# Half of the head sums moved to TensorE in a fused attention and mixture-of-experts block

## The reference

```python
scores = einsum('bhqd,bhkd->bhqk', q, k) / sqrt(DK)
attn = softmax(scores, axis=1)             # axis 1 is the HEAD axis
x = einsum('bhqk,bhkd->bhqd', attn, v)     # then times Wo
# the block: x = x + attention(layernorm(x), ctx)
#            x = x + ffn(layernorm(x))
raw = einsum('bsd,ed->bse', x, centroids)  # routing scores, top 2 of 8, softmax of the two
h_sh = gelu(x @ Wfc_sh);  shared_out = h_sh @ Wproj_sh
h_r = gelu(x @ Wfc_r);    expert_out = h_r @ Wproj_r
ffn = x + shared_out + sum over the two chosen experts of weight * expert_out
```

## Time and profile before

| | |
|---|---|
| median of 3 runs | 393.11 us (391.81 to 393.36) |
| profiled execution | 391.42 us, of which the span of the trace is 389.6 us |
| mean granted TensorE clock | 0.963 of full speed |
| TensorE busy | 317.9 us, 82% |
| VectorE busy | 282.3 us, 72% |
| ScalarE busy | 264.0 us, 68% |
| GpSimd busy | 260.4 us, 67% |

### The profile page before, as it was taken

How to read it: one execution, slowest core, us unless ns; L and a number is a source line. 1 busy time by engine, 2 the same in 40 slices (tenths; PEclk the granted TensorE clock), 3 DMA queues, 4 the chain that set the end, 5 groups by cost and what they waited for, 6 DMA issues and landing times.

```text
span 389.6 us, 11521 instructions
## 1 busy us (share of the span) xinstructions
PE 317.9 (82%) x3972; PEld 256.0 (66%) x3973; DVE 282.3 (72%) x584; ACT 264.0 (68%) x498; POOL 260.4 (67%) x268
## 2 busy tenths in 40 slices
PE   5865788566675688999999989799999999999252
PEld 1562456344454457888888666698998989999251
DVE  3789899999999979926747365667676777666255
ACT  2887799488586747565355879477676766767755
POOL 6264688789888593777777775067777777777600
PEclk9999699899989999999999999999999999999857
DMA  7957334310000000111113711413332322231098
GB/s 250 340 147 272 100 104 133 100 55 2 3 3 0 2 3 0 43 55 49 56 53 103 120 49 42 111 49 100 81 89 77 89 82 74 76 98 49 2 357 291
DMA packets 29178, 36.14 MB, mean 93 GB/s; under 512 B 4932, under 2 KB 24007, under 8 KB 28624
## 3 DMA queue, kind: packets, MB, share of 16 engines
q1 hardware_dynamic: 24592, 27.13, 23.1%
q0 software_dynamic: 4544, 8.44, 7.0%
HBM read 21.74 MB, written 14.72 MB: 94 GB/s over the span
## 4 chain that ended last, share of the span: by engine, by line
issue 27%; PE 21%; DVE 21%; POOL 16%; DMA 7%; ACT 4%; POOLq 1%; SPq 1%; DVEq 0%; ACTq 0%
POOL results L515 11%; DVE Z L931 6%; PE banks L1476 5%; DVE Mx L926 4%; POOL gathered L497 4%; DMA qRep<-results 2%; PE banks L1460 2%; PE banks L1461 2%; PE banks L1462 2%; DMA gathered<-xs,slot 2%; DMA q_rows<-qRep 1%; DVE rZ L934 1%; PE banks L1344 1%; PE banks L1354 1%; DVE stats L902 1%
## 5 line engine op out<-in xcount | busy, mean ns | idle before, releaser
L515 POOL DMA_INDIRECT results<-E,qRep x78 | 86.2, 1105 | 42.1 <-issue 28.2
L497 POOL DMA_INDIRECT gathered<-xs,slot x64 | 64.7, 1011 | 25.3 <-issue 18.6
L1212 DVE TENSOR_TENSOR E<-hid,E 128x512 f16<-128x512 f32 x78 | 54.0, 692 | 36.2 <-ACT E L780 35.9
L443 POOL TENSOR_TENSOR E<-E,rZ 128x1024 f32<-128x1024 f32 x32 | 67.5, 2131 | 17.6 <-DVE rZ L934 17.6
L778 ACT ACTIVATE hid<-banks 128x512 f32<-128x512 f32 x78 | 47.0, 603 | 38.0 <-DVE E L1212 21.0
L1576 PE MATMUL banks<-wprojL,E 128*128 x312 | 54.6, 219 | 2.9 <-DVE E L1212 1.9
L1580 PE MATMUL banks<-wprojH,E 128*128 x312 | 54.3, 219 | 0.0
L1578 PE MATMUL banks<-wprojH,E 128*128 x312 | 54.3, 219 | 0.0
L639 ACT ACTIVATE E<-banks 128x1024 f32<-128x1024 f32 x32 | 33.1, 1094 | 21.2 <-PE banks L1344 21.2
L780 ACT ACTIVATE E<-banks 128x512 f16<-128x512 f32 x78 | 47.3, 606 | 0.0
L1562 PE MATMUL banks<-qRep,wfcH 128*128 128x256 f16 x156 | 42.6, 273 | 0.7 <-ACT E L780 0.5
(11 more groups left out here) (223 smaller groups left out, 828.7 us busy)
## 6 DMA issues: line engine op xcount, KB each, us to landing
qRep<-gathered SPq DMA_DIRECT2D x39, 129.0 KB, 2.2
qRep<-q_rows SPq DMA_DIRECT2D x32, 128.0 KB, 2.6
qRep<-results SPq DMA_DIRECT2D x8, 512.0 KB, 6.8
X<-in_x SPq DMA_DIRECT2D x4, 512.0 KB, 6.7
q_rows<-qRep SPq DMA_DIRECT2D x8, 256.0 KB, 2.1
out<-X SPq DMA_DIRECT2D x8, 256.0 KB, 3.7
results<-E,qRep POOLq DMA_INDIRECT x78
gathered<-spare SPq DMA_DIRECT2D x9, 129.0 KB, 4.5
```

The source lines that it names most:

```text
L443: g.tensor_tensor(heads, heads, rZ[:, k % 2, :].unsqueeze(1).unsqueeze(3).broadcast_to([P, HH // 2, P, 2]), ALU.mult).then_inc(attn_ready, 1)
L497: g.indirect_dma_start(out=gathered, out_offset=bass.IndirectOffsetOnAxis(ap=slot[:, k, i:i + 1], axis=0), in_=xs[:, i, :], in_offset=None ...
L515: g.indirect_dma_start(out=results, out_offset=bass.IndirectOffsetOnAxis(ap=xg[:, k, h, 2 * D:ROW].bitcast(I32), axis=0), in_=yg[:, k, h, ...
L1212: v.tensor_tensor(gL[:, j, 2 * c:2 * c + 2], hid[:, 2 * j + c].rearrange("p (c q) -> p c q", c=2), gH[:, j, 2 * c:2 * c + 2], ALU.subtract ...
```

## The change

1. For units 7 to 14 the sum over heads is split. TensorE sums head groups 0 to 3 by eight matmuls of 128x128 with the identity, into 128 columns of bank 5 (`half_sum`). VectorE reduces groups 4 to 7 (1024 values in a partition in place of 2048) and adds TensorE's part. That addition waits for `half_sum` and, since bank 5 also takes `project_out`, for the `project_out` behind it.
2. On TensorE `half_sum` stands right behind the raw scores, and `project_out` moves from behind `ffn_transposes` to right behind `half_sum`. Both stand ahead of `minus_max`.
3. The seed of pairs 4 and 5 moves from the turn of unit 15 to behind the last sums. VectorE's loop is written out.
4. GpSimd normalises only the first half of unit 15; VectorE does the second, behind the routing scores' copy. The addition of unit 14 moves from ahead of `choose(0)` to behind its reciprocal.
5. At the end pair 7 is loaded, summed and stored in two halves, with both weightings on VectorE and none on ScalarE.

```diff
@@ semaphores: late_attn, zsum_ready, zhalf_ready, last_loaded; banks @@
+        z_ps = banks[:, 5, 2 * P:3 * P]
@@ sync @@
-            for a in range(PAIRS):
-                sp.dma_start(yk[:, a].rearrange("p k t d -> p (k t d)"), rv[a]).then_inc(yk_loaded[a], 16)
+            for a in range(PAIRS):
+                if a < ALONE:
+                    sp.dma_start(yk[:, a].rearrange("p k t d -> p (k t d)"), rv[a]).then_inc(yk_loaded[a], 16)
+            halves_of = results.rearrange("(a p k h n) d -> a h p k (n d)", a=PAIRS, p=P, k=2, h=2)
+            for h in range(2):
+                sp.dma_start(yk[:, ALONE, :, 2 * h:2 * h + 2].rearrange("p k t d -> p k (t d)"), halves_of[ALONE, h]
+                             ).then_inc((yk_loaded[ALONE], last_loaded)[h], 16)
...
+            for h in range(2):
+                sp.wait_ge(combined, PAIRS - len(PE_PAIRS) + h)
+                sp.dma_start(ov[:, ALONE, h], Xo[:, ALONE, h]).then_inc(stored, 16)
@@ gpsimd, normalise @@
-                for half in range(2):
+                for half in range(1 if u == UNITS - 1 else 2):
@@ vector @@
+            def sum_heads(u, k, halved):
                 dve.wait_ge(exp_done, 2 * u + 2)
+                if halved:
+                    z = Z[:, k % 2, :]
+                    v.tensor_reduce(z, E[:, k, QUARTER:HH].rearrange("p g q o -> p q g o"), AX_XY,
+                                    ALU.add).then_inc(zhalf_ready, 1)
+                    dve.wait_ge(zhalf_ready, u - SUMMED + 1)
+                    dve.wait_ge(zsum_ready, u - SUMMED + 1)
+                    dve.wait_ge(y_ready, u - 1)
+                    v.tensor_tensor(z, z, z_ps, ALU.add).then_inc(z_ready, 1)
@@ vector, four_units @@
-                    if k == 3 and not first:
+                    if k == 3 and not (first or last):
                         deviation_seed(n - 1, not second)
-                        sum_heads(u - 1, (k - 1) % 4)
+                        sum_heads(u - 1, (k - 1) % 4, not (first or second))
-            with dve.Fori(2, PAIRS // 2) as n:
-                four_units(n, False, False)
+            four_units(2, False, False)
+            four_units(3, False, False, last=True)
@@ vector, after the units @@
             scores_in(0)
+            late_heads = E[:, 3, HH // 2:HH]
+            dve.wait_ge(rz_ready, UNITS)
+            v.tensor_tensor(late_heads, late_heads, rZ[:, 1, :].unsqueeze(1).unsqueeze(3).broadcast_to([P, HH // 2, P, 2]),
+                            ALU.mult).then_inc(late_attn, 1)
             add_attention(UNITS - 3, 1, PAIRS - 2)
-            add_attention(UNITS - 2, 0, PAIRS - 1)
-            choose(0)
+            deviation_seed(PAIRS // 2 - 2, True)
+            choose(0, True)
@@ tensor @@
+            def half_sum(u, k):
+                pe.wait_ge(exp_done, 2 * u + 1)
+                pe.wait_ge(x_added, u - 2)
+                pe.wait_ge(z_ready, u)
+                for g in range(QUARTER):
+                    for odd in range(2):
+                        last = t.matmul(z_ps, ident[:], E[:, k, g, :, odd], start=(g == 0 and odd == 0),
+                                        stop=(g == QUARTER - 1 and odd == 1))
+                last.then_inc(zsum_ready, 1)
@@ tensor, four_units @@
                     raw_scores(u, k, 2 * n + k // 2, first and k == 0)
+                    if u > SUMMED:
+                        half_sum(u - 1, (k - 1) % 4)
+                        project_out(u - 3, (k - 3) % 4, False)
...
-                    if u >= PAIRS:
-                        project_out(u - 3, (k - 3) % 4, False)
```

More of the change, by code:

```diff
@@ L59 @@
 WHOLE = 5
+ALONE = PAIRS - 1
+SUMMED = 7
 PE_PAIRS = (1, 4)
@@ L248, in xattn_moe_kernel @@
             sem(n) for n in ("up_ready", "h_ready", "dn_ready", "acc_done"))
-        late_ready, late_added = sem("late_ready"), sem("late_added")
+        late_ready, late_added, late_attn = sem("late_ready"), sem("late_added"), sem("late_attn")
         h32_ready, hlo_ready, gh32_ready, ghlo_ready = (
@@ L254, in xattn_moe_kernel @@
         shared_high, shared_low = sem("shared_high"), sem("shared_low")
+        zsum_ready, zhalf_ready = sem("zsum_ready"), sem("zhalf_ready")
         member_ready, rank_ready, slot_ready, token2_ready, table_ready = (
@@ L266, in xattn_moe_kernel @@
         combined, combined_half = sem("combined"), sem("combined_half")
+        last_loaded = sem("last_loaded")
         diag_ready, sum_ready, copied = sem("diag_ready"), sem("sum_ready"), sem("copied")
@@ L363, in _ @@
             for a in range(PAIRS):
-                sp.dma_start(yk[:, a].rearrange("p k t d -> p (k t d)"), rv[a]).then_inc(yk_loaded[a], 16)
-            for a in range(PAIRS):
+                if a < ALONE:
[4 more added lines that the diff above has]
+                             ).then_inc((yk_loaded[ALONE], last_loaded)[h], 16)
+            for a in range(ALONE):
                 summed = sum(p <= a for p in PE_PAIRS)
@@ L945, in split_centroids, with four_units @@
                 v.tensor_tensor(centL[:], cent[:], centH[:], ALU.subtract).then_inc(rstep, 1)
-            def four_units(n, first, second):
+            def four_units(n, first, second, last=False):
                 for k in range(4):
@@ L1028, in scores_in, with choose @@
                                 ).then_inc(rneed, 1)
-            def choose(portion):
+            def choose(portion, residual=False):
                 lo, hi = PORTIONS[portion]
@@ L1050, in choose @@
                 then(v.reciprocal(rt[:, 4, t], rt[:, 2, t]))
+                if residual:
+                    add_attention(UNITS - 2, 0, PAIRS - 1)
                 pick(rt[:, 4, t], 5, 0)
@@ L1236, in _ @@
             dve.wait_ge(gate_ready, 2)
-            for n, a in enumerate(a for a in range(PAIRS) if a not in PE_PAIRS):
+            for n, a in enumerate(a for a in range(ALONE) if a not in PE_PAIRS):
                 dve.wait_ge(yk_loaded[a], 16)
@@ L1247, in _ @@
                 v.tensor_tensor(xv, xv, yk[:, a, 1].rearrange("p t d -> p (t d)"), ALU.add).then_inc(combined, 1)
+            others = ALONE - len(PE_PAIRS)
+            for h in range(2):
+                dve.wait_ge((yk_loaded[ALONE], last_loaded)[h], 16)
+                for k in range(2):
+                    for i in (2 * h, 2 * h + 1):
+                        xv = X[:, ALONE, h, i % 2, :]
+                        last = v.scalar_tensor_tensor(xv, yk[:, ALONE, k, i],
+                                                      gate[:, k, ALONE * TP + i:ALONE * TP + i + 1], xv, ALU.mult, ALU.add)
+                    if k == 0:
+                        last.then_inc(combined_half, 1)
+                        dve.wait_ge(combined_half, others + h + 1)
+                    else:
+                        last.then_inc(combined, 1)
         @block.tensor
@@ L1347, in minus_max @@
                         last.then_inc(s_ready, 1)
+            def half_sum(u, k):
[7 more added lines that the diff above has]
+                last.then_inc(zsum_ready, 1)
             def weighted_values(u, k, half):
-                pe.wait_ge(attn_ready, 2 * u + half + 1)
+                if u == UNITS - 1 and half:
+                    pe.wait_ge(late_attn, 1)
+                else:
+                    pe.wait_ge(attn_ready, 2 * u + half + 1)
                 for odd in range(2):
```

10 lines of the change are left out of this document (5 added, 5 removed).

## The result

The changed kernel takes 389.82 us (median of 22 runs, 387.61 to 392.42), the kernel before 392.43 in the same rounds (22 runs). The ratio is 0.9929, 95% interval 0.991 to 0.9948: 2.8 us faster, between 2.0 and 3.5. The forecast was 391.2, from a gain of 1.85 us. The profiled execution took 388.82, its span is 387.0; the one before took 391.42 with 389.6.

A forecast was written before the change was run, and what follows sets the result against it. Attention looked bound by VectorE with GpSimd close behind, its gain passed on by a TensorE-bound part. -2.1 + 0.25 = -1.85 us gave 389.6 on the profiled 391.42, 391.26 on the median's scale, predicted 391.2; range 388.8 to 393.9.

The forecast's parts named there:

- main case: Whole kernel: the summed gain of 1.85 us arrives, giving 391.2, between 390.0 and 392.5; chance 0.50.
- VectorE 0.75 less a unit, 1.85 for TensorE's half sum: Sum over heads: VectorE's 2.31 us becomes 1.56 a unit; TensorE's eight matmuls take 1.85, bounds 1.78 and 2.22.
- GpSimd holds unit 10, max(13) 0.75 earlier: Units 8 to 13: GpSimd's normalising of unit 10 lets only 0.75 of about 3 us saved reach unit 13's maximum.
- max(15) 2.3, `minus_max` 1.5 earlier: Last turns: unit 15's maximum at 128.55, not 130.86; its `minus_max` at 131.65, not 133.18; last exponentials 1.5 us earlier.
- The forecast idle time ahead of max(15): VectorE in the last turn: it would show idle time before unit 15's maximum; no size given.
- The choice 3.0 earlier, TensorE's 0.6 wait goes: Choice of experts: picks start 3.0 us earlier, TensorE's 0.6 wait at the ranking goes, so scatters come 2.1 earlier.
- The late product: 0 of a bound of 0 to +0.5: VectorE's half of unit 15's normalising: waiting for GpSimd's half costs 0, bounds 0 and +0.5 us, ScalarE's copy hiding the rest.
- The tail +0.25: End of the kernel: pair 7's weightings 0.55 later, smaller last store 0.3 off, costing 0.25 us; bounds -0.4 and +1.0.
- Passed on whole between scatter and end: Behind the first scatter: scatters and TensorE carry the 2.1 us gain undiminished to the routed experts.
- A: Rival for the attention units: VectorE's saving arrives nearly whole, GpSimd's order the floor, -3.85 us, 389.3; chance 0.18.
- B: Rival for the attention units: nothing arrives, GpSimd holds units 8 to 12 and `minus_max` is late, 392.8; chance 0.20.
- C: Rival for the attention loop: TensorE's half clock makes it slower, one turn costing 2.8 us, 394.1, two 396.9; chance 0.12.

The follow-up runs named there:

- e_two: Changed kernel with TensorE summing 2 of the 8 head groups and VectorE 6; 390.46 us, 0.9959 against the kernel before.
- e_xpose: Changed kernel with TensorE's transposes of units 10, 11, 14 and 15 behind `minus_max`; 388.67 us, 0.9900 against the kernel before.
- e_sumonly: Changed kernel with seed, unit 15's second half, unit 14's addition and pair 7 as before, leaving the half sums; 1.0023 against the kernel before, other chip.
- e_nolate: Changed kernel with GpSimd normalising both halves of unit 15; 0.9943 against the kernel before, on the other chip.
- e_nosum: Changed kernel without the half sums, VectorE summing all heads in every unit; 1.0037 against the kernel before, on the other chip.
- e_nosum2: Second run of the changed kernel without the half sums, VectorE summing all heads; 0.9943 against the kernel before, on the other chip.
- e_sumonly2: Second run of the changed kernel reduced to the half sums, the later parts as before; 0.9954 against the kernel before, on the other chip.

## Why the prediction was right, point by point

The mechanism was right, and the sum somewhat too small: 1.85 against the measured 2.8 (2.0 to 3.5). In the traces the spans differ by 2.6; 0.5 of that stand ahead of the change, and the terms of the sum measured 1.81 for 1.5, 0.95 for 0.6, 0.2 lost for 0 and 0.43 lost for 0.25, together 2.1. What makes up the rest to 2.8 isn't shown. The median of 389.82 lies 0.2 below the main case's own bounds (390.0 to 392.5); part of that is scale, since the kernel before came out at 392.43 and not at 393.11. By its steps, from GpSimd's unit 8:

- *VectorE 0.75 less a unit, 1.85 for TensorE's half sum.* Measured 1.21 + 0.29, and 1.92. Right.
- *GpSimd holds unit 10, max(13) 0.75 earlier.* 0.82. Right. But this holds only while VectorE saves the whole 0.75: in `e_two` max(13) is 1.2 later.
- *max(15) 2.3, `minus_max` 1.5 earlier.* 2.50 and 1.81. The first is right within 0.2 and the second within 0.3, but with one wrong reason: the prediction had the loop through `minus_max` set the last turn, at 6.35, where its own figure for such a turn was 6.65. Measured, the loop is 6.1 to the end of the raw scores, and VectorE's list, 6.3 long, set the turn: `e_xpose` shortened the loop by 0.4 (its raw scores of unit 15 end at 127.73, 5.7 behind its max(14) at 122.04) and the turn stayed, `e_two` lengthened the list and the turn grew by as much. The forecast idle time ahead of max(15) is missing.
- *The choice 3.0 earlier, TensorE's 0.6 wait goes.* The picks start 3.50 earlier. From `minus_max` to the scatter 0.95 are gained (23.14 to 22.19) and not 0.6: 0.14 by the last projection (13.53 and 13.39 behind `minus_max`), the rest between it and the ranking (17.75 and 16.82), where TensorE had waited. With the 0.3 of the step above, this is the term that was sized too small. That the late half was needed for it is wrong: `e_sumonly` and `e_nolate` have it without. VectorE's earlier last sums are enough for GpSimd to be done before the choice.
- *The late product: 0 of a bound of 0 to +0.5.* The rule of the Trainium skill on VectorE and GpSimd (SBUF — State Buffer, Who interferes with whom) agrees with the traces: in all ten that have this product it ended 1.07 to 1.09 behind GpSimd's last half, however early it had started. But ScalarE's copy was not all that stood behind it. TensorE's projection did, by way of VectorE's addition, and with the stretch at half clock behind it the scatter came up to 2.8 late.
- *The tail +0.25.* 0.43 in the trace, 0.3 by the means of the tails. Right in sign.
- *Passed on whole between scatter and end.* 0.2 of 2.76 lost. Right.

Of the rivals, A (389.3) lies nearest in time. It has the last turns right, since VectorE's list sets them and VectorE has no gap there, and the rest wrong: its 4.1 up to the scatter were 2.76, and `minus_max` is late as the main case has it. B is out. C, the half clock, did not come in the loop; the change took such a stretch away, worth 0.35 to 0.6 by the estimate above, which the sum had not counted. C had priced one such turn at 2.8; no run shows that price in a kernel with half sums. The half clock did come in three of the experiments, at a place that I had not named. The Trainium skill (TensorE: Matmul & The Clock Gate, What's actually happening) says that activity releases the throttle. The eleven traces with half sums agree, none of them under 1.00 between 84 and 132; of the three without, two are.

What stays open: how often a run of the kernel before has the half clock at 112, and the time of each part of the change, which the other chip's runs don't tell apart. The runs point to a version that was not run: half sums and transposes behind `minus_max`, GpSimd normalising all of unit 15, pair 7 whole. Of those that ran, `e_xpose` has the lowest ratio, not told apart from the changed kernel.

## What to carry to other kernels

When an engine's list is shortened in a loop, ask for each turn what is next behind it; here one turn was held by GpSimd, two by VectorE itself and the last `minus_max` by TensorE's order, and each answered to another experiment. The product that was split off to VectorE did not run beside GpSimd's (it ended 1.07 to 1.09 behind it), so its end hangs on where GpSimd's instruction happens to end: price such a split by who waits behind it, to the engine whose clock can fall. A part of a change that only hides beside a wait should be tested by leaving it out.

## What the runs showed of the hardware

- The same kernel (`e_nosum` and `e_nosum2`) fell to half clock in one execution and not in the other (0.51 and 1.00 at 92 to 95, 0.59 and 1.00 at 112 to 115). The first stretch cost nothing, the second 0.57 us.
- An 8-wide fp32 operation of VectorE took 1.71 us at 103.78 instead of 0.17 to 0.5, until GpSimd's normalising had ended (101.21 + 4.25 = 105.46, in the changed kernel). In the kernel before the same operation took 0.37, and ended with GpSimd's too (106.46 and 106.43).
- On one of two chips the stages behind the first scatter take 40 and 45 us longer, with the same instructions and the same durations of the indirect DMAs. In the first of them TensorE's granted clock was 0.81 instead of 1.00 (`e_sumonly2`, 154 to 279), and TensorE stood idle about 37 of 125 us; for 36 of these the profile names no releaser. The cause stays open.
